# Holding back attention tiles beside the comparisons of a search, on one core of a Trainium2 chip

## The chip, the core and the metric

The kernel is one program on one core of a Trainium2 chip. The core has a matrix engine (TensorE, PE in the rows; its weight loads are PEld), a vector engine (VectorE, DVE), a scalar engine (ScalarE, ACT), a general engine (GpSimd, POOL) and a queue engine that issues transfers (SyncE, SP). Each runs its own list of instructions in order and waits on semaphores. The metric is the device time of one execution in microseconds (us), lower is better.

## What is computed

One layer over x of shape (2, 4096, 256): an attention in which only some queries attend, a layer norm, a gated feed-forward block and a second layer norm. Cut to what matters here:

```python
scores = einsum('bhqd,bhkd->bhqk', q, k) * scale      # 16 heads, 4096 x 4096 each, DH = 16
sparsity = scores.max(axis=-1) - scores.mean(axis=-1)
_, top_idx = top_k(sparsity, U)                       # U = 307 queries of each head
q_sel = take_along_axis(q, top_idx[..., None], axis=2)
attn = softmax(einsum('bhud,bhkd->bhuk', q_sel, k) * scale)
out = zeros_like(q).at[bi, hi, top_idx].set(einsum('bhuk,bhkd->bhud', attn, v))
x = layernorm(x + out @ Wo + bo)
x_prev = shifted by one token
r = sigmoid((mu_r*x + (1-mu_r)*x_prev) @ W_r);  k = (mu_k*x + (1-mu_k)*x_prev) @ W_k
x = layernorm(x + r * (square(relu(k)) @ W_v))
```

## The kernel before

**Two kinds of attention work.** The maximum of every query's scores is needed for all 4096 queries of 32 heads (2 batches of 16). This is cut into 2048 *rounds* (`main(p)`, 64 for each head): a round multiplies 128 queries with 2048 keys (four matmuls of 512 columns, two into the banks C0 and C1, two into D0 or D1), ACT takes the absolute value of the C banks (L1055, two instructions) and one instruction of DVE adds the D bank and keeps the maximum (L1210). The 307 chosen queries of a head then attend to all keys in 32 *tiles*. A tile `st(g, hl, kc)` is a score matmul (L883), an exponential on ACT (L1084), a subtraction that yields the low half of the exponential (L1695 on POOL, or L1368 on DVE, as the function `side` says), and, six tiles later, `pv` with two matmuls into one accumulating bank P (L898, L899). `fin`, `otr` and `put` end a head: ACT copies the bank out (L1091), PE turns it (L908), DVE normalizes (L1375 to L1381), POOL adds a bias and scatters the rows with three indirect transfers (L1704, L1708). `gath`, `arr` and `qt` bring the next head's queries: three indirect transfers issued by POOL (L1668), seven small POOL instructions (L1461 to L1688), and a transposing transfer on SP.

**Searches.** The heads fall into 8 groups g = 0 to 7 of 5, 5, 3, 3, 5, 5, 3, 3 heads. When the last round of a group is done, `select(g)` finds the 307th largest value of each of its heads in 16 digits. A digit is three steps in three rounds: `cmp` (a comparison with count on ACT, L1075), a pause, and `cnt` with `digit` (a small matmul L841 and two DVE instructions, L1259 and L1265). Then follow `cut`, five `cum`, `rank`, `pick`, `slots`, `ob` (in all 16 DVE instructions L1341, each followed by a multiplication L1637 on POOL), `oa` (DVE L1346), `idx` (a matmul chain L871 and DVE L1355 to L1360) and two transfers that bring the indices back. `prelude(g)` gathers the group's first head.

**Who sets the order.** `schedule()` writes one list of tokens, and every engine runs its own share of that list in the list's order. In each round it takes one step of the search; then, unless `hold` is above zero, one step of attention (`att`), or, if attention has nothing to do, one step of the background (`back`: projections, values, and the feed-forward of batch 0 in the functions `f0` to `f9`). `hold` already keeps attention out of the round of a `cnt`, and of two rounds at a step that claims a bank (`ONE_BANK`). The name `P` is in `spare` when no attention is under way. After the 2048 rounds comes the tail: the search of group 7 with the tiles that are left of group 6 beside it (two steps of attention at a `cmp`, one at any other step), then group 7's 96 tiles, then the feed-forward of batch 1, which starts when all heads have been scattered. Batch 0's feed-forward starts when groups 0 to 3 are done, and group 5's attention waits for its end.

Of the kernel before, what the change touches and what calls it, by code (L numbers as in the profile page):

```python
# [56 lines left out]
def schedule():  # L57
# [3 lines left out]
    spare = ["B", "P", "D00", "D01", "D10", "D11", "C0", "C1"]  # L61
# [331 lines left out]
    hold = 0  # L393

    def with_lead(step, p):

        for i, token in enumerate(step):
            if token[0] in ("pv", "xt", "kmm", "qmm", "qtr", "val") and p + 1 < NB * H * NP:
                return step[:i] + [("lead", p + 1)] + step[i:]
        return step  # L400

    for n in range(NB * H):
        while n == 7 and "p0" not in done or n >= 15 and "p1" not in done:
            plan.extend(next(back) or [])
        if n + 1 < NB * H:
            plan.append(("head", n + 1))
        for p in range(NP):
            step = next(sel, None) or []
            if step and step[0][0] == "cnt":
                plan.append(("second", n * NP + p))  # L410
                plan.extend(step)
                step = []
                hold = 1 if "P" not in spare or "feed" in done else hold
            plan.append(("main", n * NP + p))
            if n + 1 in HEAD0 and p % 16 == 15:
                plan.append(("cap", HEAD0.index(n + 1) - 1, p // 16))
            if n + 1 < NB * H and p == 35:
                plan.append(("qload", n + 1, 0))
            plan.extend(step)
            if ("P" not in spare or "feed" in done) and any(token[0] in ONE_BANK for token in step):  # L420
                hold = 2
            if hold:
                hold -= 1
                continue
            step = next(att, None)
            if step is None:
                step = next(back, None)
            plan.extend(with_lead(step or [], n * NP + p))
        if n + 1 < NB * H:
            plan.append(("qload", n + 1, 1))  # L430
        if n + 1 in HEAD0:
            g = HEAD0.index(n + 1) - 1
            done.add(("c", g))
# [3 lines left out]
    while not set(range(len(GROUPS))) <= done:  # L437
        step = next(sel, None) or []
# [13 lines left out]
def attention_rwkv(nc, x, Wq, bq, Wk, bk, Wv, bv, Wo, bo, W_r, W_k, W_v, mu_r, mu_k, out):  # L452
    ctx = ExitStack()
    with ctx:
# [158 lines left out]

        ctx.enter_context(nc.allow_non_contiguous_dma(reason="columns, indices and maxima are small"))
        plan = schedule()

        low = {}
# [1354 lines left out]
```

## Time and profile before

| | |
|---|---|
| time, median of 3 runs | 3197.99 us (3196.73 to 3198.13) |
| the profiled execution | 3201.24 us; its span, first to last instruction, 3197.9 us |
| busy share of the span | PE 92%, DVE 90%, ACT 87%, POOL 49% |
| first and last round begin on DVE at | 63.8 us and 2903.4 us of the span |
| mean granted clock of PE | 0.981 of full speed |

A row of the timeline gives the start, the duration (from the first start to the last end where instructions are merged), engine, line, operation and tiles, the number merged, and in brackets idle time ahead of it with what ended it. Instructions of an engine overlap slightly, so what one costs its engine is read from start to start. Full PE clock is 2.4 GHz and the other level is 1.2 GHz.

### The profile page before, as it was taken

How to read it: one execution, taken by the hardware profiler on the slowest of the kernel's cores; microseconds unless marked ns; L12 is line 12 of the kernel's file. 1: busy time of each engine (PE TensorE's matmuls, PEld its weight loads, DVE VectorE, ACT ScalarE, POOL GpSimd, SP SyncE). 2: the span in 40 equal slices, each digit the busy share in tenths (PEclk: the TensorE clock that was granted, in tenths of full speed). 3: DMA queues.
4: the chain of work that ended last, by engine and by line, in shares of the span. 5: the costliest groups of instructions: out<-in, count | busy, mean ns of one | idle time of the engine just before them, and what ended most of it. 6: DMA issues, size and time to landing. Idle time of an engine off the chain costs nothing.

```text
span 3197.9 us, 55833 instructions
## 1 busy us (share of the span) xinstructions
PE 2933.5 (92%) x14524; PEld 1329.0 (42%) x14524; DVE 2863.7 (90%) x5704; ACT 2796.5 (87%) x6075; POOL 1568.3 (49%) x2785
## 2 busy tenths in 40 slices
PE   5999999998999999999999999899999899998688
PEld 3343333333333343443334454444444443444377
DVE  4999999999989998998999899989999898996567
ACT  5999999998999999899999888799998699896455
POOL 4223322224555564654446354666645663667744
PEclk8999999999999999999999999999999999998889
DMA  6325933351271223225121233122261124204122
GB/s 185 86 88 180 211 92 88 88 42 27 50 32 36 43 38 23 36 44 36 28 42 31 57 50 40 43 50 44 39 41 44 31 39 33 43 18 17 20 85 75
DMA packets 285867, 183.37 MB, mean 57 GB/s; under 512 B 182700, under 2 KB 264812, under 8 KB 281196
## 3 DMA queue, kind: packets, MB, share of 16 engines
q1 hardware_dynamic: 269004, 167.95, 29.7%
q0 software_dynamic: 14592, 9.76, 2.3%
q8 instruction: 116, 1.90, 0.3%
q14 instruction: 203, 1.66, 0.2%
q10 hardware_dynamic: 1952, 2.10, 0.2%
HBM read 120.25 MB, written 64.63 MB: 58 GB/s over the span
## 4 chain that ended last, share of the span: by engine, by line
DVE 32%; PE 26%; ACT 20%; issue 15%; POOL 3%; DMA 2%; SPq 1%; ACTq 0%; DVEq 0%; POOLq 0%
DVE JK L1210 28%; ACT AB L1055 17%; PE DP L822 7%; PE CP L812 4%; PE CP L803 4%; DVE SPr L1210 1%; PE DP L921 1%; PE PV L898 1%; PE PV L899 1%; ACT E L1084 1%; PE PV L921 1%; DMA VF<-AO 1%; PE BP L921 1%; PE BP L883 1%; DVE SCR L1346 1%
## 5 line engine op out<-in xcount | busy, mean ns | idle before, releaser
L1210 DVE CUSTOM_DVE_ANT_0 JK<-DP,AB 128x1024 bf16<-128x1024 f32 x2048 | 2460.1, 1222 | 195.0 <-DVE SPr L1210 83.1
L1055 ACT ACTIVATE AB<-CP 128x512 f32<-128x512 f32 x4096 | 2293.0, 623 | 172.1 <-PE CP L803 109.3
L822 PE MATMUL DP<-KS,QS 128*128 128x512 f16 x4096 | 1228.9, 382 | 56.6 <-DVE SPr L1210 47.9
L1695 POOL TENSOR_TENSOR SCR<-E 128x307 f16<-128x307 f32 x957 | 663.1, 706 | 445.9 <-ACT E L1084 441.5
L803 PE MATMUL CP<-KS,QS 128*128 128x512 f16 x2048 | 789.1, 385 | 52.5 <-ACT AB L1055 29.5
L812 PE MATMUL CP<-KS,QS 128*128 128x512 f16 x2048 | 789.3, 385 | 35.4 <-ACT AB L1055 0.5
L822 PEld LDWEIGHTS DP<-KS,QS 128*128 128x128 f16 x4096 | 352.1, 99 | 354.7 <-DVE SPr L1210 171.1
L1084 ACT ACTIVATE E<-BP 128x307 f32<-128x307 f32 x896 | 429.1, 479 | 27.0 <-PE BP L883 21.4
L803 PEld LDWEIGHTS CP<-KS,QS 128*128 128x128 f16 x2048 | 197.5, 96 | 523.1 <-ACT AB L1055 445.7
L812 PEld LDWEIGHTS CP<-KS,QS 128*128 128x128 f16 x2048 | 196.6, 96 | 420.3 <-ACT AB L1055 373.3
L883 PE MATMUL BP<-QT,KA 128*128 128x307 f16 x896 | 265.5, 296 | 3.5 <-DVE OG L1381 0.9
L1461 POOL TENSOR_SCALAR SCR<-SCR 128x48 f16<-128x48 f16 (+2 forms) x122 | 50.4, 413 | 293.1 <-ACT SCR L1033 175.2
L1210 DVE DVE_READ_ACCUMULATOR2_ANT SPr<- 128x1 f32 x2048 | 169.9, 83 | 0.0
L898 PE MATMUL PV<-E,XT 128*128 128x307 bf16 x512 | 159.1, 311 | 9.1 <-POOL SCR L1695 7.8
L899 PE MATMUL PV<-SCR,XT 128*128 128x307 f16 x512 | 155.4, 304 | 0.0
L898 PE MATMUL PV<-E,VF 128*128 128x307 bf16 x512 | 153.4, 300 | 0.0
L899 PE MATMUL PV<-SCR,VF 128*128 128x307 f16 x512 | 149.8, 292 | 0.0
L883 PEld LDWEIGHTS BP<-QT,KA 128*128 128x128 f16 x896 | 87.8, 98 | 134.9 <-ACT E L1084 26.5
L1668 POOL DMA_INDIRECT SCR<-QN,idxs x96 | 100.3, 1045 | 57.5 <-issue 33.0
L1708 POOL DMA_INDIRECT AO<-OG,idxs x96 | 100.8, 1050 | 33.3 <-issue 20.5
L1730 POOL TENSOR_SCALAR frs<-fmv 128x1 f32<-128x1 f32 x64 | 14.0, 219 | 147.3 <-DVE fmv L1391 147.0
L1084 ACT ACTIVATE E<-DP 128x307 f32<-128x307 f32 x99 | 40.1, 436 | 47.8 <-PE DP L883 43.7
(405 smaller groups left out, 2904.4 us busy)
## 6 DMA issues: line engine op xcount, KB each, us to landing
KS<-KTC SPq DMA_DIRECT2D x256, 128.0 KB
QS<-QSC SPq DMA_DIRECT2D x512, 64.0 KB
KA<-KTC SPq DMA_DIRECT2D x128, 128.0 KB
QN<-SCR SPq DMA_DIRECT2D x16, 544.0 KB, 3.5
SCR<-in_L_attn_x SPq DMA_DIRECT2D x16, 512.0 KB, 7.6
AO<-E SPq DMA_DIRECT2D x16, 512.0 KB, 9.3
Y<-in_L_attn_x SPq DMA_DIRECT2D x16, 512.0 KB, 9.1
Y<-bob POOLq DMA_DIRECT2D x16, 512.0 KB, 33.5
```

Of the source, the lines that this page charges most:

```text
L803: pe.matmul(o, qs, ks[0][:, 1, :], start=True, stop=True).then_inc(sc_c, 1)
L812: pe.matmul(o, qs, ks[1][:, 1, :], start=True, stop=True).then_inc(sc_c, 1)
L822: r = pe.matmul(o[:, 512 * j:512 * j + 512], qs, ks[j][:, 0, :], start=True, stop=True)
L883: pe.matmul(o[:, 0:U], KA[hx % 2][:, 128 * kc:128 * kc + 128], QT[hx % 2][:, 0:U], start=True, stop=True).then_inc(s_pe, 1)
L898: pe.matmul(PV[:, 0:U], v, EH[a % NE], start=kc == 0, stop=False)
L899: pe.matmul(PV[:, 0:U], v, EL[a % NE], start=False, stop=kc == NT - 1).then_inc(pv_pe, 1)
L1055: act.activation(AB[p % 3][:, 512 * j:512 * j + 512], BANK["C%d" % j], ACT.Abs).then_inc(ab_full, 1)
L1084: act.activation(E[a % NE][:], BANK[bank][:, 0:U], ACT.Exp, scale=2 * SCALE / (WS * WS)).then_inc(ex_act, 1)
L1210: dve.tensor_tensor_reduce(out=JK[p % 2][:], in0=BANK["D%d" % u], in1=AB[p % 3][:], scale=1.0, scalar=0.0, op0=ALU.add, op1=ALU.max, accum ...
L1668: pool.indirect_dma_start(out=QG[0:w, 3 * (hx % 8) + c, :], out_offset=None, in_=QNr[b], in_offset=bass.IndirectOffsetOnAxis(ap=ixf[0:w, k ...
L1695: pool.tensor_tensor(EL[a % NE], E[a % NE][:], EH[a % NE], ALU.subtract).then_inc(el_g, 1)
L1708: pool.indirect_dma_start(out=AOr[b], out_offset=bass.IndirectOffsetOnAxis(ap=ixf[0:w, k:k + 1], axis=0), in_=OG[i][0:w, c, :], in_offset= ...
```

## The change

In a round whose search step is a `cmp`, while attention is under way, `hold` is raised to at least 1. So no step of attention is taken in that round: neither a tile nor the `pv`, `fin`, `put` or `gath` that would have stood there.

```diff
--- before.py
+++ after.py
@@ -419,6 +419,8 @@
             plan.extend(step)
             if ("P" not in spare or "feed" in done) and any(token[0] in ONE_BANK for token in step):
                 hold = 2
+            if step and step[0][0] == "cmp" and "P" not in spare:
+                hold = max(hold, 1)
             if hold:
                 hold -= 1
                 continue
```

Four of the searches run beside attention: those of groups 1, 2, 3 and 6. Counted in the list of tokens, 60 of their 64 comparison rounds held a tile and a `pv` (three of the other four a head's end, one nothing); now none does. Of the 60, 32 go to the tail in the balance, and rounds outside comparisons hold 28 tiles more than before: 12 more rounds of `oa` and 8 more of `ob` hold a tile, and 8 other rounds. Of the list's 1024 tiles, 875 stood in rounds before and 843 now, 149 in the tail before and 181 now. Group 3's attention ends at round 1270 instead of 1251, the first `f0` stands at round 1277 instead of 1258, group 5's first tile at 1816 instead of 1797, group 6's at 2037 instead of 2002. The tail now begins with group 6's tile (hl 0, kc 11), before with (hl 1, kc 11).

**Place 1, ACT in the search of group 1.** One digit, from one comparison to the next. L1075 is the comparison, L1055 the absolute values of a round (two each), L1084 a tile's exponential. Before:

```order
L1075 ACTIVATE masks,counted<-upper_half,test 120x512
L1084 ACTIVATE E<-BP 128x307
L1055 ACTIVATE AB<-CP 128x512 x2
L1084 ACTIVATE E<-BP 128x307
L1055 ACTIVATE AB<-CP 128x512 x4
L1075 ACTIVATE masks,counted<-upper_half,test 120x512
```

And now (all lines are two further down):

```order
L1077 ACTIVATE masks,counted<-upper_half,test 120x512
L1057 ACTIVATE AB<-CP 128x512 x2
L1086 ACTIVATE E<-BP 128x307
L1057 ACTIVATE AB<-CP 128x512 x4
L1077 ACTIVATE masks,counted<-upper_half,test 120x512
```

The exponential behind the comparison is gone, the one in the pause is left: a digit has one tile instead of two.

**Place 2, POOL in the tail, digits 9 to 15 of the last search.** L1708 is the scatter of a head, L1695 a tile's subtraction, L1601 the first instruction behind the digits. Before:

```order
L1704 TENSOR_TENSOR OG<-OG,bvb 128x48
L1708 DMA AO<-OG,idxs 65536x16 x3
L1695 TENSOR_TENSOR SCR<-E 128x307 x20
L1601 MEMSET masks 128x6
L1603 MEMSET lower_half 128x96 x2
```

And now:

```order
L1710 DMA AO<-OG,idxs 65536x16 x3
L1697 TENSOR_TENSOR SCR<-E 128x307 x4
L1670 DMA SCR<-QN,idxs 128x17 x2
L1670 DMA SCR<-QN,idxs 51x17
L1697 TENSOR_TENSOR SCR<-E 128x307 x8
L1463 TENSOR_SCALAR SCR<-SCR 128x3x16 x2
L1685 TENSOR_TENSOR SCR<-SCR 128x3x16
L1463 TENSOR_SCALAR SCR<-SCR 128x3x16
L1687 TENSOR_SCALAR MH<-SCR 128x3
L1689 CAST SCR<-MH 128x3
L1690 TENSOR_TENSOR SCR<-MH,SCR 128x3
L1697 TENSOR_TENSOR SCR<-E 128x307 x8
```

The 20 subtractions are the same in number, and one head's gather (L1670) and its arranging (L1463 to L1690) now stand among them.

**Place 3, POOL in the tail, from the digits' end to the gather of group 7.** L1637 is the multiplication of the `ob` steps. Before:

```order
L1695 TENSOR_TENSOR SCR<-E 128x307 x6
L1461 TENSOR_SCALAR fa<-upper_half 128x96
L1461 TENSOR_SCALAR fb<-lower_half 128x96
L1637 TENSOR_TENSOR SCR<-SCR,tokc 128x96 x16
L1704 TENSOR_TENSOR OG<-OG,bvb 128x48
L1708 DMA AO<-OG,idxs 65536x16 x3
L1668 DMA SCR<-QN,idxs 128x17 x2
L1668 DMA SCR<-QN,idxs 51x17
```

And now, from the instruction behind the two on `fa` and `fb`:

```order
L1697 TENSOR_TENSOR SCR<-E 128x307
L1639 TENSOR_TENSOR SCR<-SCR,tokc 128x96 x4
L1697 TENSOR_TENSOR SCR<-E 128x307
L1639 TENSOR_TENSOR SCR<-SCR,tokc 128x96 x4
L1697 TENSOR_TENSOR SCR<-E 128x307
L1639 TENSOR_TENSOR SCR<-SCR,tokc 128x96 x4
L1697 TENSOR_TENSOR SCR<-E 128x307
L1639 TENSOR_TENSOR SCR<-SCR,tokc 128x96 x4
L1706 TENSOR_TENSOR OG<-OG,bvb 128x48
L1710 DMA AO<-OG,idxs 65536x16 x3
L1697 TENSOR_TENSOR SCR<-E 128x307 x5
L1670 DMA SCR<-QN,idxs 128x17 x2
```

Four subtractions now stand among the 16 multiplications and five more ahead of the gather. Behind the gather and its arranging the list now has eight more subtractions on POOL (others go to DVE), the scatter of group 6's last head, and only then the subtraction of group 7's first tile; before, that one stood directly behind the arranging.

## Rows read from the trace of the kernel before

**Rows 1.** The chain that ended last, shares of the span by engine.

```profile
DVE 32%; PE 26%; ACT 20%; issue 15%; POOL 3%; DMA 2%; SPq 1%; ACTq 0%; DVEq 0%; POOLq 0%
```

**Rows 2.** L1210 alone by stretches: start:end, length, DVE busy (instructions, two a round), clock, transfers.

```profile
662.82:730.55 67.73, 57.42 (x97) 1.00 0.43 10
922.95:996.55 73.60, 57.58 (x97) 1.00 0.68 18
1602.52:1620.80 18.28, 18.11 (x33) 1.00 0.24 36
894.05:910.90 16.85, 16.00 (x26) 1.00 0.18 33
```

**Rows 3.** Timeline of ACT, one digit of group 1's search, tiles beside it.

```profile
940.72 0.72 ACT L1075 ACTIVATE masks<-upper_half,test 120x512 bf16<-120x512 int32 x1
...
941.42 0.42 ACT L1084 ACTIVATE E<-BP 128x307 f32<-128x307 f32 x1
941.73 1.09 ACT L1055 ACTIVATE AB<-CP 128x512 f32<-128x512 f32 x2
...
944.33 1.09 ACT L1055 ACTIVATE AB<-CP 128x512 f32<-128x512 f32 x2 [0.21 <-PE CP L803]
945.29 0.72 ACT L1075 ACTIVATE masks<-upper_half,test 120x512 bf16<-120x512 int32 x1
```

**Rows 4.** Timeline of ACT, one digit of group 0's search, no tiles.

```profile
670.48 0.72 ACT L1075 ACTIVATE masks<-upper_half,test 120x512 bf16<-120x512 int32 x1
...
672.14 0.40 ACT L1049 ACTIVATE SCR<-BP 128x256 f32<-128x256 f32 x1
672.40 1.11 ACT L1055 ACTIVATE AB<-CP 128x512 f32<-128x512 f32 x2
...
674.70 0.72 ACT L1075 ACTIVATE masks<-upper_half,test 120x512 bf16<-120x512 int32 x1
```

**Rows 5.** Timeline of DVE and POOL, `ob` steps of group 2's search.

```profile
1301.15 0.28 DVE L1341 TENSOR_SCALAR SCR<-fb 128x96 f16<-128x96 f16 x2
...
1302.19 1.10 POOL L1668 DMA_INDIRECT SCR<-QN,idxs  x1 [0.30 <-issue]
...
1304.36 2.95 DVE L1341 TENSOR_SCALAR SCR<-fb 128x96 f16<-128x96 f16 x2
```

**Rows 6.** Timeline of POOL in the tail, digits to the arranged queries.

```profile
2939.63 13.15 POOL L1695 TENSOR_TENSOR SCR<-E 128x307 f16<-128x307 f32 x20
...
2960.85 6.89 POOL L1637 TENSOR_TENSOR SCR<-SCR,tokc 128x96 f16<-128x96 f16 x16 [0.31 <-DVE SCR L1341]
2967.70 0.28 POOL L1704 TENSOR_TENSOR OG<-OG,bvb 128x48 f32<-128x48 f32 x1
...
2970.89 1.08 POOL L1708 DMA_INDIRECT AO<-OG,idxs  x1 [0.30 <-issue]
2975.59 1.00 POOL L1668 DMA_INDIRECT SCR<-QN,idxs  x1 [3.62 <-DMA idxs<-IDX]
...
2978.15 1.09 POOL L1668 DMA_INDIRECT SCR<-QN,idxs  x1 [0.31 <-issue]
2980.79 0.54 POOL L1461 TENSOR_SCALAR SCR<-SCR 128x48 f16<-128x48 f32 x2 [1.55 <-DMA SCR<-QN,idxs]
...
2982.39 0.20 POOL L1688 TENSOR_TENSOR SCR<-MH,SCR 128x3 f16<-128x3 f32 x1
```

**Rows 7.** Timeline of PE in the tail, group 7's first head.

```profile
2985.06 0.41 PE L883 MATMUL DP<-QT,KA 128*128 128x307 f16 x1 [15.35 <-DMA QT<-SCR]
...
2986.99 0.42 PE L898 MATMUL PV<-E,XT 128*128 128x307 bf16 x1
...
2996.09 0.31 PE L898 MATMUL PV<-E,XT 128*128 128x307 bf16 x1 [1.94 <-POOL SCR L1695]
...
3003.19 0.34 PE L908 MATMUL BP<-ident,OT 33*128 33x33 f32 x3 [0.69 <-ACT OT L1091]
```

**Rows 8.** Timeline of DVE in the tail, the last digit's count.

```profile
2948.87 0.17 DVE L1259 SCALAR_TENSOR_TENSOR hits<-DP,worth 72x9 f32<-72x9 f32 x1 [0.71 <-PE DP L841]
```

## The prediction

> **What bounds the kernel now.** I read the page first. By the chain that ended last, no one engine bounds the kernel: DVE, PE and ACT hold 32%, 26% and 20% of it [rows 1]. So a cost has to be read stage by stage. In the rounds I looked at L1210 alone, because one pair of its instructions is one round. Where nothing else is done a round takes 18.28 us / 16 = 1.14 us with DVE busy all through (33 instructions in the stretch, half a round more; the third row) [rows 2]: DVE is the bound. With one tile in each round it takes 16.85 / 13 = 1.30 us and DVE waits a little (the fourth row) [rows 2]. So a tile in a round that would else be free costs 1.30 - 1.14 = 0.16 us, although it occupies ACT for twice that: the rest lies in ACT's slack under DVE.
>
> The search of group 1, with two tiles to a digit, takes 73.60 us for its 48 rounds, that of group 0, with none, 67.73 us [rows 2]. The timeline of ACT shows why. From comparison to comparison are 945.29 - 940.72 = 4.57 us and ACT runs through but for 0.21 us; the comparison costs 941.42 - 940.72 = 0.70 us, and the exponential behind it 941.73 - 941.42 = 0.31 us [rows 3]. Here ACT is the bound, and that exponential is paid in full. In the tail POOL is the busy engine beside the last search: 20 subtractions in 13.15 us without a gap, 0.66 us each [rows 6]. Behind that search PE stands idle for 15.35 us until the queries of group 7 have landed [rows 7].
>
> **The change part by part.** It adds and removes no instruction; it moves tiles, and with them ends and gathers of heads.
>
> *The comparison rounds.* 60 tiles leave them. With the exponential gone a digit should fall from 4.57 to 4.57 - 0.31 = 4.26 us. A row supports it from the other side: a digit of group 0 without tiles, but with one eviction of 672.40 - 672.14 = 0.26 us on ACT in the pause, takes 674.70 - 670.48 = 4.22 us [rows 4]; with the 0.31 us of an exponential in that place it would be 4.27. That is the form a digit has now. So 0.31 us a tile where ACT is full. As an upper bound 60 x 0.31 = 18.6 us; where something hides a part, a tile is worth no less than the 0.16 us of a plain round, 9.6 us. I take 17.5, near the upper end, since the two rows are of just this place. Digits are not delayed by it: the chain comparison, count, digit stands where it stood.
>
> *The 28 tiles that find other rounds.* Eight plain rounds at 0.16 us: 1.3 us. Of the 12 in `oa` and 8 in `ob` rounds, DVE has more to do there, so a tile costs between nothing and 0.16 us each, 0 to 3.2; I take 1.7. Sum 3.0 us.
>
> *Collisions at `ob`.* The gather of a head now falls among the `ob` steps of group 1's search, where none did, and leaves those of group 2. In group 2 before, two L1341 took 2.95 us, just behind such a gather, against 0.28 for a pair before it [rows 5]: 2.7 us lost, once. One collision comes and one goes; and group 3's `ob` steps, formerly without tiles, now have some. I take +0.5 us, with -3 and +6 as ends.
> The Trainium skill ("SBUF — State Buffer", Who interferes with whom) says that such a `tensor_scalar` and a GpSimd instruction exclude each other by a lock held for one whole instruction, the later one blocking. By that a wait is at most one GpSimd instruction, and the sum would have nothing for the collisions; the pair of 2.95 us is longer than any one POOL instruction near it, so here the trace doesn't agree with so small a price.
>
> *In the rounds* the sum is -17.5 + 3.0 + 0.5 = **-14 us** (ends -19 and -7). The feed-forward of batch 0 begins 19 rounds later; it has the same steps, fills the rounds up to group 5's attention as before, and costs nothing by that. What it does is push tiles out at the end, into the tail.
>
> *The tail.* Its first subtractions, the group's stored maxima and the wait for queries come at the same steps as before, one head earlier. Then POOL decides. Its list has, one behind the other:
> 1. A gather and an arranging among digits 10 to 15 (place 2). A gather costs POOL 2978.15 + 1.09 - 2975.59 = 3.7 us, an arranging 2982.39 + 0.20 - 2980.79 = 1.8 us [rows 6]. The digits wait for it: PE takes each count behind a `pv`, whose subtraction comes every 3 x 0.66 = 1.97 us, which is the digits' own pace, and POOL has no gap. The last count, at 2948.87 [rows 8], moves by 5.5 us.
> 2. Four subtractions among the 16 multiplications (place 3): 4 x 0.66 = 2.6 us. The others before them fill POOL's idle time. So POOL ends them at 2967.7 + 5.5 + 2.6 = 2975.8.
> 3. The scatter, 2970.89 + 1.08 - 2967.70 = 4.3 us, and five subtractions, 3.3 us: 7.6 us. The gather of group 7 had waited from 2967.70 to 2975.59, 7.9 us, for the index chain and its transfer. So this costs nothing; without the cover it would be 3.3 us. The gather starts at 2983.7, and its queries are arranged 7.0 us later [rows 6], at 2990.7 instead of 2982.6.
> 4. In front of group 7 stand 20 tiles of group 6 and the `pv` of 26. PE can do ten `pv` while POOL gathers, then it meets one whose subtraction stands behind the arranging. The `pv` of 16 tiles are left at 2991.4. The 16 from 2996.09 on took about 6.1 us, until 0.98 us before 3003.19 [rows 7]. At the lower clock it is more: I take 7.5 us, so 2998.9.
> 5. The end of that head: 1.0 us to L908 [rows 7], some 1.3 us to DVE's result, 4.3 us of scatter, and 0.7 us for the first subtraction of group 7, which stands behind the scatter on POOL. Before, this scatter lay in the shadow of the index chain. The first `pv` of group 7 starts at 2998.9 + 7.3 = 3006.2 instead of 2986.99 [rows 7].
>
> That is **+19 us** at this point. From there on POOL and PE have the same list as before; seven tiles of group 7 have been started in advance, which wins nothing, since PE waits 1.94 us for POOL at the seventeenth [rows 7], as it will again. Ends: +15, if the head's end overlaps the last tiles, and +23, if PE runs them at the low clock throughout.
>
> *Sum:* -14 + 19 = +5 us. The profiled execution of 3201.24 would become 3206.2; that lies 3.25 us above the median of the timed runs, so the forecast is 3198.0 + 5 = **3203 us**. A difference under 0.2%, 6.4 us, is about what a measurement of this kernel can't tell from no change.
>
> **Rivals.**
> *A, the tail swallows most of it (faster).* PE has 15.35 us of idle time behind the last search [rows 7], and 20 tiles are put just there. If the arranging isn't in the way, as when POOL's gather and PE's tiles fully overlap, only the delay of the digits and multiplications is left, 8.1 us, and with -17.5 in the rounds the time is 3198 - 9 = 3189. It decides where the tail costs less than the rounds give by 6.4 us, that is under 8 us. Against it: the order on POOL, with eight subtractions behind the arranging and the scatter ahead of group 7. Chance 0.12.
> *B, POOL collisions in the rounds (slower).* The new gather among `ob` steps of five heads, where DVE does longer L1341 than with three, costs one or two stalls of 2.7 us, group 3's new tiles another, and the tail costs 21: -10 + 21 = +11, so 3209. For it speaks the pair of 2.95 us [rows 5]; it decides when the rounds give back less than 13 us with a tail of 19. Chance 0.33.
> *C, ACT isn't what paced a digit.* The chain comparison, count, digit then keeps 4.57 us and the rounds give nothing: -0 + 3 + 19 = +22, 3220. Group 0's 4.22 us [rows 4] speaks against it. Chance 0.05.
> *The forecast,* rounds -14, tail +19, has 0.50. From these cases: faster by over 0.2% 0.12; within it 0.49, the most of the forecast's case and a little of B; slower 0.39, B, C and the rest of the forecast's, whose middle of +5 lies near the bound of 6.4. The range reaches to A at 3190 and past B to 3214, leaving C out; the forecast's own range is 3198 to 3209.
>
> **What would show it.** In the profile after: a digit of group 1's search of about 4.26 us on ACT, with no L1086 right behind L1077; rounds without anything still 1.14 and with a tile 1.30 us. The last round begins on DVE near 2903.4 - 14 = 2889. From there to the last digit's count 5.5 us more than the 45.5 us of before; PE's 15.35 us wait gone, and shorter waits for POOL in its place, one of them some 6 us before group 7's first `pv`; from that `pv` to the end 211 us, as before. It is wrong if the digits in the tail are not paced by POOL, if the new place of a gather stalls DVE for more than one pair of L1343, or if the feed-forward of batch 0 meets a new wait by starting 19 rounds later.

## The result: slower by 0.43%

The changed kernel takes 3212.56 us, the median of 5 executions (3209.63 to 3219.2), against 3197.74 us for 5 of the kernel before on the same chip. The ratio is 1.0043 with a 95% interval of 1.0031 to 1.0054. So the change costs 14.8 us by the medians. The forecast was 3203 us: the time lies 9.6 us above the point, on the side of "slower", and 1.4 us inside the upper end of the range, 3214.

The profiled execution of after is the fastest of its five, 3209.63 us with a span of 3207.9 us, and that of before lay above its median. So the two traces differ by 10.0 us of span where the medians differ by 14.8. What follows accounts for the 10.0; the other 4.8 come back below.

From the page of after: the span, the busy times and the chain by engine.

```profile
span 3207.9 us, 55832 instructions
...
PE 2947.5 (92%) x14524; PEld 1335.2 (42%) x14524; DVE 2875.6 (90%) x5717; ACT 2800.9 (87%) x6075; POOL 1562.9 (49%) x2772
...
DVE 34%; ACT 21%; PE 21%; issue 15%; POOL 5%; SPq 2%; DMA 2%; ACTq 0%; DVEq 0%; POOLq 0%
```

The shares of busy time are as before. In the chain, PE loses 5 points against [rows 1]; DVE and POOL gain 2 each, ACT and SP's queue 1 each.

The rounds, sorted by what stands in them (a round runs from one L1210 or L1212 on DVE to the next; all 2048 are summed from the trace):

| us | before | after | difference | forecast |
|---|---|---|---|---|
| start-up, to the first round | 63.8 | 62.4 | -1.4 | 0 |
| the 80 rounds with a comparison | 135.9 | 118.0 | -18.0 | -17.5 |
| the 309 with a step of the feed-forward | 489.1 | 499.2 | **+10.1** | 0 |
| the 90 of `ob` and `oa` | 143.4 | 144.3 | +0.9 | with the next row |
| all others | 2071.2 | 2071.1 | -0.1 | +3.5 |
| the tail, from the start of the last round | 294.5 | 312.9 | **+18.4** | +19 |

(The forecast of +3.0 for tiles in other rounds and +0.5 for collisions stands in the fifth row.) So one term, which was set to nothing, is 10 us, and the others hold within 3 us.

**The comparison rounds.** The stretch of group 1's search, L1212 alone, and one digit of it on ACT, of after:

```profile
921.90:990.80 68.90, 57.44 (x97) 1.00 0.63 12
```

```profile
938.35 0.72 ACT L1077 ACTIVATE masks<-upper_half,test 120x512 bf16<-120x512 int32 x1
939.05 1.08 ACT L1057 ACTIVATE AB<-CP 128x512 f32<-128x512 f32 x2
940.01 0.45 ACT L1086 ACTIVATE E<-BP 128x307 f32<-128x307 f32 x1
940.31 1.11 ACT L1057 ACTIVATE AB<-CP 128x512 f32<-128x512 f32 x2
941.64 1.08 ACT L1057 ACTIVATE AB<-CP 128x512 f32<-128x512 f32 x2 [0.21 <-PE CP L805]
942.61 0.72 ACT L1077 ACTIVATE masks<-upper_half,test 120x512 bf16<-120x512 int32 x1
```

Right behind the comparison no exponential stands any more, and the digit is 942.61 - 938.35 = 4.26 us long, against 4.57 [rows 3]. The idle 0.21 us is the same one. The 48 rounds take 68.9 us against 73.6 [rows 2].

**The feed-forward.** Round 1690 takes 8.49 us; the same round of before 1.55. SP's queue and PE of after, just ahead of it:

```profile
2345.02 11.25 SPq L1898 DMA_DIRECT2D QN<-S  x8
...
2358.08 12.41 SPq L1898 DMA_DIRECT2D QN<-S  x8
2370.59 1.70 SPq L1935 DMA_DIRECT2D VF<-Y  x1
2372.33 0.61 SPq L1936 DMA_DIRECT2D VF<-AO  x1
```

```profile
2371.11 0.38 PE L710 MATMUL PV<-ident,VF 128*128 128x128 f32 x2
2377.91 0.66 PE L710 MATMUL BP<-ident,VF 128*128 128x128 f32 x2 [6.42 <-DMA VF<-AO]
```

L1898 stores the one column of group 5's query table in pieces of 4 bytes, a step named `sel`, one in each of the search's first five comparison rounds, with four transfers. Each transfer holds SP for 12.41 / 8 = 1.6 us. L1935 and L1936 load the next 128 rows of the feed-forward. They stand behind 16 of the 20 stores (before, behind 12), land late, and PE waits 6.42 us; the rounds wait with it. The same queue and the same load of before:

```profile
2371.90 5.26 SPq L1896 DMA_DIRECT2D QN<-S  x4
2377.26 1.31 SPq L1933 DMA_DIRECT2D VF<-Y  x1
2378.61 0.43 SPq L1934 DMA_DIRECT2D VF<-AO  x1
2379.09 10.69 SPq L1896 DMA_DIRECT2D QN<-S  x8
```

```profile
2386.35 0.38 PE L708 MATMUL PV<-ident,VF 128*128 128x128 f32 x2
```

Here the load is issued 2386.35 - 2378.61 = 7.7 us before PE comes to it. In after it is issued 1.2 us later than PE comes to it. Such a load lands 6.0 to 6.5 us after its issue in these two stretches (medians), so the 7.7 us of before were hardly more than enough. The trace of before even has such a wait, in round 1287, where no store stands ahead:

```profile
1814.53 0.66 PE L708 MATMUL BP<-ident,VF 128*128 128x128 f32 x2 [3.58 <-DMA VF<-AO]
```

Two more rounds are long, 1783 (5.23 us) and 1808 (4.68 us). PE of after in both, each with a row of POOL:

```profile
2521.24 1.10 POOL L1670 DMA_INDIRECT SCR<-QN,idxs  x1 [0.30 <-issue]
...
2526.20 0.86 PE L923 MATMUL BP<-W_rT,VF 128*128 128x256 f32 x2 [3.22 <-POOL VF L1771]
...
2566.13 0.23 POOL L1644 TENSOR_SCALAR S<-S 128x48 f32<-128x48 f32 x1 [1.16 <-DVE S L1226]
...
2567.62 1.19 PE L923 MATMUL PV<-W_vT,VF 128*128 128x256 f32 x2 [2.40 <-POOL VF L1781]
```

In the first, POOL's share of the feed-forward stands behind the gather of group 5's first head; in the second, behind a copy of the maxima (L1644) that waits for DVE. Before, rounds 1783 and 1808 took 2.60 and 1.15 us, and 1785, where the gather met a later step, took 3.86 us against now 1.33.

**The tail.** POOL of after, from the digits with the gather among them to group 7's first subtraction:

```profile
2935.92 5.29 POOL L1697 TENSOR_TENSOR SCR<-E 128x307 f16<-128x307 f32 x8
...
2955.97 0.70 POOL L1697 TENSOR_TENSOR SCR<-E 128x307 f16<-128x307 f32 x1
...
2964.39 1.28 POOL L1639 TENSOR_TENSOR SCR<-SCR,tokc 128x96 f16<-128x96 f16 x4
2965.62 0.29 POOL L1706 TENSOR_TENSOR OG<-OG,bvb 128x48 f32<-128x48 f32 x1
...
2969.97 3.56 POOL L1697 TENSOR_TENSOR SCR<-E 128x307 f16<-128x307 f32 x5
2973.70 1.05 POOL L1670 DMA_INDIRECT SCR<-QN,idxs  x1 [0.17 <-issue]
...
2981.03 0.20 POOL L1690 TENSOR_TENSOR SCR<-MH,SCR 128x3 f16<-128x3 f32 x1
...
2992.04 0.29 POOL L1706 TENSOR_TENSOR OG<-OG,bvb 128x48 f32<-128x48 f32 x1 [2.77 <-DVE OG L1383]
...
2996.69 0.71 POOL L1697 TENSOR_TENSOR SCR<-E 128x307 f16<-128x307 f32 x1
```

And PE, with its waits for POOL around the end of group 6's last head; then DVE's last count:

```profile
2981.95 0.44 PE L900 MATMUL PV<-E,XT 128*128 128x307 bf16 x1 [5.81 <-POOL SCR L1697]
...
2990.83 0.34 PE L910 MATMUL DP<-ident,OT 33*128 33x33 f32 x3 [0.67 <-ACT OT L1093]
...
2997.54 0.41 PE L900 MATMUL PV<-E,XT 128*128 128x307 bf16 x1 [5.09 <-POOL SCR L1697]
```

```profile
2944.32 0.17 DVE L1261 SCALAR_TENSOR_TENSOR hits<-DP,worth 72x9 f32<-72x9 f32 x1 [2.11 <-PE DP L843]
```

The gather of group 7 follows the fifth subtraction without a wait for its indices (0.17 us, where before POOL waited 3.62 us for them [rows 6]): POOL is now the late one. PE's 15.35 us behind the search [rows 7] have become 5.81 and 5.09 us, as tiles fill the rest, and the first `pv` of group 7 stands at 2997.54.

### The profile page after: what moved, and what is told of

Its sections match the earlier page's. It is cut to its first block, busy times and chain, and to the rows that moved or that the text cites. A ratio compares the mean times of both kernels' runs of the same rounds, so it can differ in the third digit from the quotient of the medians.

```text
span 3207.9 us, 55832 instructions
## 1 busy us (share of the span) xinstructions
PE 2947.5 (92%) x14524; PEld 1335.2 (42%) x14524; DVE 2875.6 (90%) x5717; ACT 2800.9 (87%) x6075; POOL 1562.9 (49%) x2772
## 4 chain that ended last, share of the span: by engine, by line
DVE 34%; ACT 21%; PE 21%; issue 15%; POOL 5%; SPq 2%; DMA 2%; ACTq 0%; DVEq 0%; POOLq 0%
DVE JK L1212 30%; ACT AB L1057 19%; PE DP L824 5%; PE CP L814 3%; PE CP L805 3%; DVE SPr L1212 2%; PE DP L923 1%; SPq L1898 1%; PE BP L923 1%; POOL SCR L1697 1%; PE PV L923 1%; DMA VF<-AO 1%; PE PV L900 1%; PE PV L901 1%; ACT E L1086 1%
## 5 line engine op out<-in xcount | busy, mean ns | idle before, releaser
L1212 DVE CUSTOM_DVE_ANT_0 JK<-DP,AB 128x1024 bf16<-128x1024 f32 x2048 | 2459.7, 1222 | 180.3 <-DVE SPr L1212 68.4
L824 PE MATMUL DP<-KS,QS 128*128 128x512 f16 x4096 | 1229.2, 382 | 52.5 <-DVE SPr L1212 45.5
L1086 ACT ACTIVATE E<-BP 128x307 f32<-128x307 f32 x876 | 421.7, 481 | 40.4 <-PE BP L885 37.1
L1463 POOL TENSOR_SCALAR SCR<-SCR 128x48 f16<-128x48 f16 (+2 forms) x122 | 50.8, 416 | 291.6 <-ACT SCR L1035 174.3
L1212 DVE DVE_READ_ACCUMULATOR2_ANT SPr<- 128x1 f32 x2048 | 169.2, 83 | 0.0
L1670 POOL DMA_INDIRECT SCR<-QN,idxs x96 | 100.1, 1042 | 34.3 <-issue 31.4
L1086 ACT ACTIVATE E<-DP 128x307 f32<-128x307 f32 x119 | 49.2, 428 | 40.5 <-PE DP L885 39.6
```

Of the source, the lines that this page charges most:

```text
L824: r = pe.matmul(o[:, 512 * j:512 * j + 512], qs, ks[j][:, 0, :], start=True, stop=True)
L1086: act.activation(E[a % NE][:], BANK[bank][:, 0:U], ACT.Exp, scale=2 * SCALE / (WS * WS)).then_inc(ex_act, 1)
L1212: dve.tensor_tensor_reduce(out=JK[p % 2][:], in0=BANK["D%d" % u], in1=AB[p % 3][:], scale=1.0, scalar=0.0, op0=ALU.add, op1=ALU.max, accum ...
L1670: pool.indirect_dma_start(out=QG[0:w, 3 * (hx % 8) + c, :], out_offset=None, in_=QNr[b], in_offset=bass.IndirectOffsetOnAxis(ap=ixf[0:w, k ...
```

## Experiments

Theory N says that the missing 10 us are new waits of the batch-0 feed-forward, which starts 19 rounds later; theory T that the tail carries the loss, because POOL does the moved tiles' subtractions in a row. A rival to both is that holding back attention shifts something in the rounds that no single wait shows. Each kernel was timed against the kernel before on its own chip, so ratios can be compared between runs, medians only roughly.

### The rule for group 6 alone

```diff
-            if step and step[0][0] == "cmp" and "P" not in spare:
+            if step and step[0][0] == "cmp" and "P" not in spare and step[0][1] == 6:
```

> Holds attention back beside the comparisons of group 6's search alone; batch 0's feed-forward keeps its rounds. Theory (three separate terms: 0.32 us for each tile out of a comparison round, about 10 us for the later feed-forward, and a tail paced by POOL): group 6's digits fall from 4.48 to 4.16 us, the feed-forward rounds take 489 us as before, the tail has 13 tiles more and takes 6 to 10 us more, the sum is +1 to +6 us. Rival (what the feed-forward lost belongs to the held comparisons or to chance): the feed-forward's rounds differ by several us here too.

Measured: 3200.43 us, ratio 1.0002 (0.9992 to 1.0012), which is +0.6 us where +1 to +6 were expected. The rounds give 7.1 us back (comparisons -4.3, `ob` and `oa` -2.7), the feed-forward's are unchanged (488.9), and the tail takes 300.1 us, 5.6 more (6 to 10 were expected), with 13 tiles more in it. Group 6's search comes after the feed-forward, so there nothing is displaced, and no gain or loss can be told from the times.

### The rule for groups 1 to 3 alone

```diff
-            if step and step[0][0] == "cmp" and "P" not in spare:
+            if step and step[0][0] == "cmp" and "P" not in spare and step[0][1] < 6:
```

> Holds attention back beside the comparisons of groups 1 to 3 alone, so that batch 0's feed-forward starts 19 rounds later and the tail has 16 tiles more. Theory: comparison rounds give 13 to 14 us back, the feed-forward loses about 10, the tail 7 to 10; sum +3 to +8 us. Rival (the stalls of the feed-forward are chance): the feed-forward's rounds take 489 us, sum -7 to -3.

Measured: 3208.29 us, ratio 1.0028 (1.0016 to 1.0041). Comparison rounds -13.2, feed-forward's +8.3 (round 1690 takes 6.03 us), tail +9.5 with 16 tiles more. The two halves add up to the whole only roughly: comparisons -4.3 - 13.2 = -17.5 (whole -18.0), feed-forward -0.2 + 8.3 = 8.1 (10.1), tail 5.6 + 9.5 = 15.1 (18.4, but with 32 tiles more where the halves have 13 + 16 = 29). In this trace the rounds called "all others" are 5.2 us longer too, which the whole doesn't show; what lengthens them stays open. The new stalls come from groups 1 to 3, as they do if the delayed start is their cause.

### The kernel before, feed-forward begun 19 rounds later

```diff
-        for _ in range(5):
+        for _ in range(24):
```

Applied to the kernel before: the comparisons keep their tiles, only the wait of rounds ahead of `f0` is longer.

> The kernel before, with its feed-forward of batch 0 begun 19 rounds later by 24 pauses instead of 5 and nothing held back. Its tail has the same tokens as that of the run with groups 1 to 3. Theory (the shift alone costs): digits stay 4.57 and 4.48 us, the feed-forward's rounds take about 10 us more with the stalls at rounds 1690 and 1808, the tail 7 to 10 more, 16 tiles fewer in rounds give 2 back; sum +14 to +19 us. Rival: feed-forward unchanged, sum +5 to +8.

Measured: 3217.18 us, ratio 1.0052 (1.0038 to 1.0065). The digits are as before (4.57 us). The feed-forward's rounds take 6.8 us more, with the same three long ones: 1690 takes 7.68 us, 1783 4.86, 1808 3.80. PE at round 1690:

```profile
2391.76 0.66 PE L708 MATMUL BP<-ident,VF 128*128 128x128 f32 x2 [5.60 <-DMA VF<-AO]
```

So the later start alone makes these stalls, whatever stands beside a comparison. The tail is 11.3 us longer too (7 to 10 were expected): the attention of groups 5 and 6 begins later, and 16 fewer rounds hold a tile (859 against 875). Rounds and tail together cost 4.7 + 11.3 = 16.0 us more in the trace, and nothing in this kernel gives them back.

### A tile moved from the comparison to the count

```diff
-                hold = 1 if "P" not in spare or "feed" in done else hold
+                hold = 1 if "P" in spare and "feed" in done else hold
```

Applied to the changed kernel, in the branch of a `cnt`: the tile kept out of the comparison round may stand beside the count.

> As the changed kernel no attention step in a comparison's round, but one in the count's round, where the kernel before holds it back: two tiles a digit as before, no tile moved to the tail, the feed-forward where it was. Theory (what ACT has to do in a digit bounds it: 3 x 0.95 + 0.70 + 2 x 0.31 = 4.2 us at least, 4.57 measured with its waits): a digit stays within 4.35 and 4.6 us and the sum is -8 to +2 us. Rival (the place beside the comparison is what costs, because the count waits there): a digit of 4.2 to 4.3 us, sum -20 to -14 us.

Measured: 3247.44 us, ratio 1.0153 (1.0139 to 1.0168). The feed-forward (488.9) and the tail (294.7) are as before, but a digit of group 1's search takes 5.30 us, and both expectations of it missed. PE, DVE and ACT of this kernel at a count:

```profile
942.22 0.38 PE L843 MATMUL BP<-blocks,counted 120*120 120x15 f32 x2
...
943.34 0.27 DVE L1267 TENSOR_SCALAR test<-test,hits,ahead_of 120x1 f32<-120x1 f32 x1
...
943.67 0.30 PE L885 MATMUL BP<-QT,KA 128*128 128x307 f16 x1 [0.63 <-DVE test L1267]
...
944.07 0.43 ACT L1086 ACTIVATE E<-BP 128x307 f32<-128x307 f32 x1 [0.93 <-PE BP L885]
```

The tile's scores go to the same bank BP as the count's sum, and PE writes it only when DVE is done with the sum (0.63 us of waiting). DVE turns to the sum only behind its round. Then ACT, which paces the digit, waits 0.93 us. A count round goes from 1.14 to 2.07 us; a tile there costs three times what it costs beside a comparison. For the question asked the run shows one thing: with no tile lost to the rounds, the feed-forward starts where it did and is not slowed.

### The changed kernel with the stores spread out

```diff
-            yield [("cmp", g, i, on)] + ([("sel", g, i)] if i < n else [])
+            yield [("cmp", g, i, on)] + ([("sel", g, i // 2)] if i % 2 == 0 and i // 2 < n else [])
```

The same stores, but in every second comparison round.

> The changed kernel with the stores of a search's maxima (sel, four transfers a head) at every second digit instead of at every digit. Theory (the wait of 6.4 us for VF<-AO at round 1690 is because SP takes 16 such stores, 1.4 us each, ahead of that load): eight stores are ahead of it now, round 1690 takes under 3 us instead of 8.49, the feed-forward's rounds fall by 5 to 8 us, and the sum against the kernel before falls from +14 to about +7 us. Rival (the transfer engines as such are late there): round 1690 keeps 6 us or more.

Measured: 3204.34 us, the median of nine executions, ratio 1.0026 (1.0015 to 1.0037); a tenth, of 5689 us, is left out. SP and PE of this kernel at round 1690:

```profile
2353.54 4.45 SPq L1898 DMA_DIRECT2D QN<-S  x4
2358.09 1.77 SPq L1935 DMA_DIRECT2D VF<-Y  x1
2359.91 0.43 SPq L1936 DMA_DIRECT2D VF<-AO  x1
```

```profile
2372.97 0.38 PE L710 MATMUL PV<-ident,VF 128*128 128x128 f32 x2
2373.19 0.38 PE L710 MATMUL BP<-ident,VF 128*128 128x128 f32 x2
```

The load is issued 13 us before PE comes to it, PE does not wait, and round 1690 takes 1.55 us. The feed-forward's rounds fall from 499.2 to 492.6, 3.5 above before; rounds 1783 and 1808 stay long (5.11 and 4.55), as is to be expected if POOL is their cause.

### The same in the kernel before

The edit of the run above, applied to the kernel before.

```diff
-            yield [("cmp", g, i, on)] + ([("sel", g, i)] if i < n else [])
+            yield [("cmp", g, i, on)] + ([("sel", g, i // 2)] if i % 2 == 0 and i // 2 < n else [])
```

> The kernel before with the stores of the maxima at every second digit, as a control. Theory: no 6 us wait of the feed-forward behind them is there to remove; feed-forward's rounds 489 us within 2; the tail's wait of 5.7 us for the transposing transfer behind them may shrink by 1 to 5 us; sum -6 to 0 us. Rival: the stores also slow the feed-forward before, so its rounds fall by 5 us or more.

Measured: 3196.82 us, ratio 1.0003 (0.9995 to 1.0012), round 1690 1.55 us as before, the feed-forward's rounds 489.7 us. The tail is 4.2 us shorter in the trace (290.3 us), as was thought possible, but the times show no gain. So the stores don't slow the feed-forward of the kernel before, and what the run above gained there is a repair of the change's own damage.

### The changed kernel, tiles beside comparisons in the tail on DVE

```diff
-            return "G"
+            return "D" if tail[0] and state.get("beside") else "G"
...
-        for _ in range(2 if step and step[0][0] == "cmp" else 1):
+        for k in range(2 if step and step[0][0] == "cmp" else 1):
+            state["beside"] = k == 0 and bool(step) and step[0][0] == "cmp"
...
+            state["beside"] = False
```

In the last search, the first tile behind each comparison has its subtraction on DVE instead of POOL.

> The changed kernel, and beside the last search the first tile behind each comparison takes its subtraction from DVE instead of POOL (15 of 48). Theory (POOL paces that stretch, DVE has 0.7 us idle behind each comparison): the 5.5 us that a gather and an arranging add among the digits go, the tail falls from 312.9 to 300 to 306 us. Rival (PE or the digits' own chain paces it): the tail stays above 310 us, or grows, since DVE's chain of the digits gets 0.48 us longer a digit.

Measured: 3198.19 us, ratio 1.0006 (0.9997 to 1.0015). The tail takes 307.3 us, 5.6 less than that of after and a little outside the 300 to 306 expected: the last count comes 4.8 us earlier, at 44.6 us behind the last round's start, and the first `pv` of group 7 at 96.8 instead of 102.6. Against the ratio of after that is a gain of 0.37%, some 12 us, more than the tail's share. In its trace the rounds are 5.2 us shorter as well, 4.2 of them in round 1690, which takes 4.32 us here though nothing was done about it. So the tail's share of the gain is some 6 us; the rest isn't shown to come from the edit.

### The same in the kernel before

```diff
-            return "G"
+            return "D" if tail[0] and state.get("beside") else "G"
```

with the same three lines in the loop.

> The kernel before, with the first tile behind each comparison of the last search subtracted on DVE, as a control. Theory: POOL is paced by the digits here nearly as much as it paces them, so the tail falls from 294.5 by 2 to 5 us only. Rival (POOL is all that holds the tail up): 7 us or more; (DVE's chain paces it): it grows.

Measured: 3190.74 us against 3195.42 of the kernel before on that chip, ratio 0.9988 (0.9979 to 0.9996). The tail is 287.1 us, 7.4 less than before, where 2 to 5 were expected: the rival, 7 us or more, holds. So POOL holds up the tail of either kernel, and the edit shortens the tail of before no less than that of after. It is a gain of its own and doesn't need the change.

### The changed kernel, group 7's first tile on DVE

```diff
+        if g + 1 == len(GROUPS) and (hl, kc) == (0, 0):
+            return "D"
```

> The changed kernel with the subtraction of group 7's first tile on DVE, so that the first pv of group 7 no longer stands behind the last scatter of group 6 on POOL. Theory (the scatter costs 4.3 us on the path): the first pv of group 7 comes 4 to 5 us earlier after the last round. It reaches the end only if POOL's own list lets it: the next gather and the seventeenth tile still stand behind the scatter, so the time from that pv to the end grows by 3 to 5 us and the tail keeps 311 to 313 us. Rival (the first tile alone held group 7): the tail falls to 309 us or less.

Measured: 3213.26 us, ratio 1.0046 (1.0032 to 1.0061). PE of this kernel at the two ends of the gap (its lines are two further down):

```profile
2990.28 0.34 PE L912 MATMUL DP<-ident,OT 33*128 33x33 f32 x3 [0.67 <-ACT OT L1095]
...
2992.12 0.30 PE L902 MATMUL PV<-E,XT 128*128 128x307 bf16 x1 [0.20 <-DVE SCR L1372]
```

From the turning of group 6's last head to the first `pv` of group 7 it is 1.84 us instead of 6.71: point 5 of the forecast's tail sees the scatter rightly. But from that `pv` to the end it is 215.5 us instead of 210.4, so the gain is given back and the tail stays at 313.4 us, as expected: the next subtractions and group 7's second gather stand behind the scatter on POOL all the same.

### Both edits, on before, on group 6 alone, and on the changed kernel

The stores spread and the tail's tiles on DVE, in three kernels. The edits are those above; the second kernel has besides

```diff
+            if step and step[0][0] == "cmp" and "P" not in spare and step[0][1] == 6:
+                hold = max(hold, 1)
```

Kernel before with both:

> The kernel before with both repairs, stores at every second digit and the first tile behind a comparison of the last search on DVE. The two gave 4.2 and 7.4 us in the tail each alone. Theory (they remove different waits, of PE for the transposing transfer and of PE for POOL): 283 to 286 us in the tail, sum -5 to -11 us against the kernel before. Rival (both remove the same wait): 287 to 290 us.

Group 6's rule with both:

> Both repairs, and attention held back beside the comparisons of group 6 alone. The held comparisons gave about 7 us in the rounds and took 5.6 in the tail (first run). Theory (with POOL relieved the 13 tiles more cost less than 5.6): tail 286 to 290 us, and 2 to 5 us faster than with the repairs alone. Rival: tail 5 us or more longer than with the repairs alone, no gain.

Changed kernel with both:

> The changed kernel with both repairs. Theory: the feed-forward's rounds take 491 to 495 us instead of 499, the tail 302 to 307 instead of 313, so against the kernel before 0 to +3 us, and against the kernel before with the same repairs +8 to +12 us: what is left is the tail's price of 32 tiles and three stalls of the later feed-forward. Rival (the loss was these two waits alone): equal to the kernel before with the repairs, or faster.

Measured on one chip (the kernel before at 3199.24 us, 31 executions):

| | median | ratio, interval | feed-forward's rounds | tail |
|---|---|---|---|---|
| before with both | 3195.29 | 0.9987, 0.9977 to 0.9997 | 487.9 | 286.8 |
| group 6's rule with both | 3195.72 | 0.9992, 0.9981 to 1.0002 | 489.7 | 295.4 |
| changed with both | 3200.41 | 1.0006, 0.9997 to 1.0016 | 493.5 | 305.6 |

The first lies where the DVE edit alone had brought it, its tail between the 283 to 286 us of its theory and the 287 to 290 of its rival: the gains don't add. The second gains nothing over the first, and its rival holds, not the theory of a tail of 286 to 290 us: in their traces the rounds are 10.5 us shorter and the tail is 8.6 us longer, and the medians are 0.4 us apart. The changed kernel falls from 1.0043 to 1.0006, no lower than with the DVE edit alone. Its feed-forward's rounds and its tail are as expected, but it stays 5 us behind before with both, where 8 to 12 were expected. So with the repairs the rule costs 5 us instead of 14.8, and no version with it beats the one without.

## Why the prediction came out as it did

**The comparison rounds (-17.5) were right.** They give 18.0 us. The digit is 4.26 us, to the hundredth what the forecast built from [rows 3] and [rows 4]. In groups 2, 3 and 6 it falls from 4.48 to 4.16 us. Rival C, that ACT doesn't pace a digit, is ruled out.

**Tiles in other rounds and collisions (+3.5) came to less, +0.8.** Three rounds of group 1's search, two of `ob` and one of `oa`, now take 3.15, 2.95 and 3.06 us, where the forecast had one such. The forecast had the collision in group 2's leave; its gather only moves ahead of the first pair, and the round of 4.01 us there becomes one of 3.56. One of 3.41 elsewhere is gone. (13 more rounds of `oa` hold a tile and 7 others, not 12 and 8.) Together the `ob` and `oa` rounds cost 0.9 us, so rival B has its stalls but not its price. DVE of after in group 1's `ob` steps, and POOL beside them:

```profile
1025.04 2.09 DVE L1343 TENSOR_SCALAR SCR<-fb 128x160 f16<-128x160 f16 x2
...
1034.20 0.30 DVE L1343 TENSOR_SCALAR SCR<-fb 128x160 f16<-128x160 f16 x2
1035.56 1.89 DVE L1343 TENSOR_SCALAR SCR<-fb 128x160 f16<-128x160 f16 x2
```

```profile
1023.75 1.08 POOL L1710 DMA_INDIRECT AO<-OG,idxs  x1 [0.30 <-issue]
1024.85 0.71 POOL L1697 TENSOR_TENSOR SCR<-E 128x307 f16<-128x307 f32 x1
1025.50 0.91 POOL L1639 TENSOR_TENSOR SCR<-SCR,tokc 128x160 f16<-128x160 f16 x2
1026.38 0.69 POOL L1697 TENSOR_TENSOR SCR<-E 128x307 f16<-128x307 f32 x1
...
1034.02 1.11 POOL L1670 DMA_INDIRECT SCR<-QN,idxs  x1 [0.30 <-issue]
```

The first pair behind POOL's three indirect transfers (a scatter ahead of the one, a gather ahead of the other) loses 1.6 to 1.8 us, and the five pairs between lose 0.3 us at most. The Trainium skill ("SBUF — State Buffer", Who interferes with whom) says that a `tensor_scalar` in a two-port mode and a GpSimd instruction exclude each other, the later one blocked until the first has finished. By that no wait would be longer than one POOL instruction. Here one L1343 alone takes 1.57 us, against 0.19 us for the median of the 16, and the POOL instructions at its side take 0.71 us at most; it ends 0.1 us behind the second subtraction after its start. So the trace doesn't agree with the size, and other pairs beside the same kind of POOL instructions hardly wait. No run shows which mode L1343 runs in.

**The step that failed is the sentence that the feed-forward "costs nothing by that".** The forecast counted its steps, found them equal, and didn't ask which transfers its loads now stand behind on SP. The end of that part even names this as what would make it wrong. From the first round to round 1656 after gains 15.2 us on before, with group 6's comparisons still to come, where the forecast had 14 for all rounds together; between rounds 1656 and 1816 it loses 12.8, and by the last round 7.1 are left. The runs show the rest: only kernels whose `f0` begins 19 rounds later, by either means, have the stalls; with the stores spread the one of round 1690 is gone. Its size varies from trace to trace. In five kernels with that order round 1690 takes 8.49, 7.68, 6.03, 4.32 and 4.17 us, and in all nine others 1.55. The 16 stores ahead of the load vary as well: they take 11.25 + 12.41 = 23.7 us where PE waits longest, and 9.96 + 10.70 = 20.7 us in the kernel with 4.32 us, where PE waits 2.36. What makes them vary stays open. The stalls of rounds 1783 and 1808 are the same in all with the late start (4.9 to 5.6 and 3.8 to 4.7 us). No run moved POOL's copy or the gather, so that these two are POOL's is read from the waits, not tried.

**The tail (+19) was right in sum, less in its steps.**

| behind the last round's start, us | before | after | difference | forecast |
|---|---|---|---|---|
| last digit's count | 45.5 | 49.4 | +3.9 | +5.5 |
| last multiplication of `ob` | 64.3 | 70.7 | +6.4 | +8.1 |
| group 7's queries arranged | 79.2 | 86.3 | +7.1 | +8.1 |
| first `pv` of group 7 | 83.6 | 102.6 | +19.0 | +19.2 |
| the end | 294.5 | 312.9 | +18.4 | +19 |

The last count moved by 3.9 us and not by 5.5: the digit that waits for a head's transposing transfer takes 5.38 instead of 7.61 us (PE waits 3.85 us there instead of 5.67), and that hides a part. Four subtractions among the multiplications cost 2.5 us, as forecast (2.6). Then the 16 `pv` behind the arranging take until 2990.16, 8.2 us from 2981.95 where the forecast had 7.5: the first seven come 0.77 us apart, at a granted clock of 0.50 behind PE's wait, the next two 0.4 and the last seven 0.27, at 1.00; and the head's end takes 7.4 us where it had 7.3. These are small misses of both signs, and that they nearly cancel is luck. Rival A, that PE's idle time swallows the tiles, is out: the limit was POOL's list, as the DVE edit shows. Its price of 3189 was also too low by its own terms, since it left out the +3.5 us of the other rounds.

**Chances and point.** With the feed-forward's 10 us in place, the forecast's sum is 3213 us. The case that came true (a gain of 7 in the rounds and a tail of 18) was priced near rival B, for another reason. That the time lies in the stated range is therefore luck in part: it is outside the 3198 to 3209 that the forecast's own mechanism allowed, and only the room left for rival B takes it in. "Slower" had 0.39, and that was too little: a shift of all later work by 19 rounds was priced at zero with no spread, and of the forecast's own range (0 to +11 us) four tenths already lay above the bound of 6.4 us. Of the 14.8 us in the medians, the traces explain 10.0. The profiled execution of after is 2.9 us below its median and that of before was 3.5 us above this batch's, 6.4 us in all, against 1.6 us by which times differ less than spans; together they make the 4.8. That is only the arithmetic of it: which stage varies so between executions stays open. From trace to trace round 1690 alone varies by 4 us, and the first round starts between 61 and 69 us.

## What to carry to other kernels

Work held back in one place starts everything behind it later, so walk each queue, SP's too, past the new place of every load, and ask what small transfers it now stands behind; a step with an equal count of instructions can still be 10 us dearer. What is saved in the busiest rounds (0.3 us a tile here, 18 us for 60) is paid back where the leftovers end up (18.4 us for 32 of them, 0.6 us each), so price the last stage by the engine that paces it, here POOL. And where an engine is to be relieved, move work to another engine there (DVE, 5.6 and 7.4 us of the tail) before moving it to another time.

## What the runs showed of the chip

- A transfer with pieces of 4 bytes holds SP's queue 1.1 to 1.6 us each (L1898: eight in 12.41 us, four in 4.45 us), one with whole rows 0.4 us, or 1.3 to 1.9 us right behind such stores (L1935, 1.70 us). 16 of the stores take 11.25 + 12.41 = 23.7 us ahead of a load behind them, and the load lands some 6 us after its issue.
- Two small instructions of DVE (0.30 us) take 1.9 to 2.1 us just behind three indirect transfers of POOL (2.95 us in the kernel before), and 0.3 to 0.6 us in the pairs between, beside the same kind of POOL work.
- A filler matmul that shares a bank with a short chain across three engines costs 0.93 us each time on the engine that waits last (ACT).
- Two traces with the same order up to that round differ by 4 us in a single one that waits for a transfer (8.49 and 4.17 us).
